# Banded attention in a two-layer decoder kernel: projections in three rounded terms, weights streamed by group, and a new order of the work

## The reference

```python
x = x + _L0_attn_ref(_layernorm(x), wq, wk, wv, wo)

q = einsum('bth,oh->bto', x, wq).reshape(B, T, 16, 128)
k = einsum('bth,oh->bto', x, wk).reshape(B, T, 4, 128)
v = einsum('bth,oh->bto', x, wv).reshape(B, T, 4, 128)
q, k = rope(q), rope(k)
scores = q @ k / sqrt(128)             # keys 128 back at most, none ahead
probs = softmax(scores)
out = (probs @ v).reshape(B, T, 2048) @ wo.T
```

## Time and profile before

| | |
|---|---|
| median of 3 runs | 2411.59 us (2409.08 to 2414.42) |
| the profiled execution | 2406.55 us, span of its trace 2404.8 us |
| attention stage in that trace | 8.6 to 928.6 us |
| busy over the whole span: PE, DVE, ACT, POOL | 89%, 71%, 39%, 44% |
| the same from 0 to 930 us | 92%, 75%, 34%, 38% |

### The profile page before, as it was taken

One profiled execution on the slowest core, in us unless ns is written; L12 is line 12 of the kernel. 1 busy time (PEld: TensorE's weight loads), 2 busy tenths in 40 slices (PEclk: granted clock), 3 DMA queues, 4 the chain that ended last, 5 costly groups with the idle time before them and its releaser, 6 DMA issues. The chain is left out here.

```text
span 2404.8 us, 24923 instructions
## 1 busy us (share of the span) xinstructions
PE 2151.0 (89%) x7344; PEld 1108.7 (46%) x7344; DVE 1712.6 (71%) x2983; ACT 944.7 (39%) x1808; POOL 1048.7 (44%) x798
## 2 busy tenths in 40 slices
PE   6998999899999977997889898999789999999858
PEld 2554445454455543443555555465333433334234
DVE  1787788768876885786889889889546364654554
ACT  1443344333333433764655646465123232332311
POOL 2343354333333440322899998999511011010142
PEclk9999999999999998998999999999889999999979
DMA  7000000000000002455644526353332122221121
GB/s 263 19 19 18 19 20 20 18 18 22 22 18 19 23 23 90 159 186 214 266 162 166 197 105 210 127 203 108 107 80 78 41 77 57 70 70 46 52 109 53
DMA packets 95563, 214.87 MB, mean 89 GB/s; under 512 B 15832, under 2 KB 33112, under 8 KB 93032
## 3 DMA queue, kind: packets, MB, share of 16 engines
q1 hardware_dynamic: 77192, 156.18, 19.8%
q10 hardware_dynamic: 17760, 57.42, 6.7%
q0 software_dynamic: 512, 0.13, 0.0%
HBM read 146.30 MB, written 42.07 MB: 78 GB/s over the span
## 5 line engine op out<-in xcount | busy, mean ns | idle before, releaser
L759 POOL TENSOR_SCALAR a_prob<-a_prob,a_rsum 128x256 f32<-128x256 f32 x256 | 146.6, 590 | 467.3 <-DVE a_rsum L687 467.1
L1455 POOL TENSOR_TENSOR s_state<-s_b_rows,s_delta_u 128x1024 f32<-128x1024 f32 x128 | 303.5, 2384 | 36.9 <-DMA s_b_rows<-scan_bc 34.4
L1499 DVE TENSOR_TENSOR_SCAN s_state<-s_decay,s_state 128x512 f32<-128x512 f32 x256 | 304.9, 1211 | 15.5 <-ACT s_decay L1441 13.2
L1614 PE MATMUL c_bank<-c_xn_parts,c_w_parts 128*128 128x512 f32 (+1 forms) x1056 | 269.5, 405 | 6.2 <-DMA c_w_parts<-ffn_weights_lo 6.2
L1441 ACT ACTIVATE s_decay<-s_delta,s_a 128x512 f32<-128x512 f32 x256 | 173.5, 689 | 226.1 <-DVE s_state L1499 220.6
L491 PE MATMUL a_bank<-a_xn_t,a_wq 128*128 128x512 f32 x512 | 227.3, 592 | 0.0
L602 ACT ACTIVATE a_prob<-a_score,a_neg_m 128x256 f32<-128x256 f32 x256 | 117.6, 475 | 279.0 <-DVE a_neg_m L682 278.8
L1614 PEld LDWEIGHTS c_bank<-c_xn_parts,c_w_parts 128*128 128x128 f32 (+1 forms) x1056 | 196.3, 187 | 65.8 <-issue 20.3
L574 PE MATMUL a_bank<-a_wo,a_out_t 128*128 128x512 f32 x512 | 222.3, 593 | 0.0
L2049 ACT ACTIVATE d_prob_t<-d_score 128x512 f32<-128x512 f32 x256 | 138.9, 595 | 192.2 <-PE d_score L1931 191.1
L373 DVE TENSOR_SCALAR f_picks<-f_mask,f_lut_xor,f_lut 128x260 int32<-128x260 int32 x512 | 202.3, 468 | 9.6 <-DVE f_mask L367 0.5
(11 more groups left out here) (210 smaller groups left out, 3646.2 us busy)
## 6 DMA issues: line engine op xcount, KB each, us to landing
s_b_rows<-scan_bc SPq DMA_DIRECT2D x64, 512.0 KB, 3.7
c_w_parts<-ffn_weights_hi ACTq DMA_DIRECT2D x39, 512.0 KB, 3.6
c_w_parts<-ffn_weights_lo ACTq DMA_DIRECT2D x39, 512.0 KB, 4.5
f_idx<-in_idx SPq DMA_DIRECT2D x64, 130.0 KB, 2.1
ffn_weights<-f_picks SPq DMA_DIRECT2D x64, 130.0 KB, 1.8
d_qs<-d_hi SPq DMA_DIRECT2D x128, 64.0 KB, 2.0
d_ks<-d_hi SPq DMA_DIRECT2D x128, 64.0 KB, 2.0
d_factor<-in_factors SPq DMA_DIRECT2D x16, 512.0 KB, 3.6
```

The lines of the kernel that those rows point to most:

```text
L1455: pool.tensor_tensor(self.state[:, s], row.broadcast_to([P, 2, T]), self.delta_u[:, h % 2], ALU.mult) \
L1499: dve.tensor_tensor_scan(self.state[:, s, e, :], self.decay[u % 2][:], self.state[:, s, e, :], 0.0, ALU.mult, ALU.add).then_inc(self.scann ...
L1614: mm = nc.tensor.matmul(banks[b][0:width[o], :], w_parts[:, n % SLOTS, w, at:at + width[o]], xn_parts[:, x_, k, :], start=((k, w, x_) == t ...
```

## The change

**Split projections.** Wk, Wq and Wv and the transposed x are each held as two float32r parts, the value rounded (`hi`) and what is left (`lo`). A projection into one bank is then 12 float32r matmuls, hi x hi, lo x hi and hi x lo over four row blocks, in place of four float32 ones. Scores, weighting and output product stay float32.

**Streamed weights.** `HeadWeights` holds the parts of one group at a time (five pieces: k and four q; 512 KB with both parts). In the first pass each piece is loaded raw (256 KB, two buffers), rounded by ACT, subtracted by POOL and stored to DRAM by SP; afterwards SP loads the parts of group g + 2 as soon as PE has used those of group g + 1. The values' weights go the same way once. The key's pieces are multiplied by 1/sqrt(128) before rounding, so the exponential loses its scale, and the maximum is taken with its sign turned, so line 682 goes.

**New order.** PE: scores 0 and 1, two projections, scores 2 and 3, three projections, then the output product of the group before (in group 0 the values of this row), then the weighting. In group 3: scores, xn transposes, output of group 2, projections of the next row, weighting, output of group 3. DVE, ACT and POOL follow; the features are now rounded by ACT and subtracted by DVE. The chunks are dealt 4, 4, 3, 5 to the groups. All DMAs of the stage go through SP, in one order with the lookup's. The first pass is unrolled.

```diff
+    GROUPS = (0, 4, 8, 11, PER_PASS)
...
+class HeadWeights:
...
+    def load_piece(self, sp, m, source):
+        if m >= 2:
+            sp.wait_ge(self.split, m - 1)
+        sp.dma_start(self.raw[:, m % 2, :], source).then_inc(self.raw_in[m % 2], 16)
+
+    def load_raw(self, sp, n, p):
+
+        if n:
+            sp.wait_ge(self.stored[p], 16 * n)
+        self.load_piece(sp, self.piece(n, p), self.dram["head_w"][:, n * self.STEPS + p, :])
...
+    def store(self, sp, n):
+        for p in range(self.STEPS):
+            sp.wait_ge(self.ready[p], 16 * (n + 1))
+            sp.dma_start(self.scratch["head_parts"][:, n * self.STEPS + p], self.parts[:, p].bitcast(F32)) \
+                .then_inc(self.stored[p], 16)
...
+    def round(self, act, n, steps):
+        for p in steps:
+            m = self.piece(n, p)
+            if p == 0:
+                raw = self.raw[:, m % 2, :]
+                act.wait_ge(self.raw_in[m % 2], 16 * (m // 2 + 1))
+                self.nc.scalar.activation(raw, raw, ACT.Copy, scale=1.0 / math.sqrt(HD)).then_inc(self.scaled, 1)
+                act.wait_ge(self.scaled, n + 1)
+            self.round_piece(act, m, self.parts[:, p, 0, :])
+
+    def subtract(self, pool, n, steps):
+        for p in steps:
+            m = self.piece(n, p)
+            pool.wait_ge(self.rounded, m + 1)
+            self.nc.gpsimd.tensor_tensor(self.parts[:, p, 1, :], self.raw[:, m % 2, :],
+                                         self.parts[:, p, 0, :].bitcast(F32), ALU.subtract) \
...
-            if g + 1 < KV:
-                order += proj(g + 1)
...
+            if g < LAST:
+                order += proj(g + 1) + (wo_steps(g - 1) if g else v_steps)
             elif more:
-                order += xn_steps + proj(0)
+                order += xn_steps + wo_steps(g - 1) + proj(0)
...
+            def one_pass(i, more):
+                first_pass, last_pass = (isinstance(i, int) and i == at for at in (0, B - 1))
+                for g in range(KV):
+                    chunks = lookup.chunks(g)
+                    ahead = 3 if g == LAST else 1
+                    lookup.sync(sp, i, chunks[:ahead])
+                    if first_pass and g == 0:
+                        for k in range(1, KD):
+                            load_values(k)
+                        load_outputs(0)
+                    if first_pass and g == 1:
+                        for b in range(1, B):
+                            sp.dma_start(x[:, b], dram["x"][b].rearrange("(t p) d -> p t d", p=P)).then_inc(x_in, 16)
+                        load_outputs(2)
+                        load_outputs(3)
+                    if first_pass and g < LAST:
+                        heads.store(sp, g + 1)
+                    if not last_pass or g + 2 < KV:
+                        for p, step in enumerate(proj((g + 1) % KV)):
+                            consumed(ring, i, step)
+                            if first_pass and g < LAST and p == REPS:
+                                lookup.sync(sp, i, chunks[1:2])
+                            if first_pass and g + 2 < KV:
+                                heads.load_raw(sp, g + 2, p)
+                            else:
+                                heads.load_parts(sp, (g + 2) % KV, p,
+                                                 after_stores=KV if first_pass and g + 2 == KV else None)
+                    if first_pass and g == 0:
+                        load_outputs(1)
+                    lookup.sync(sp, i, chunks[2 if first_pass and g < LAST else ahead:])
...
+                for g in range(LAST):
                     scores(i, g, (0, 1))
...
+                    project(ring, i, i, g + 1, proj(g + 1)[0:2])
+                    scores(i, g, (2, 3))
+                    project(ring, i, i, g + 1, proj(g + 1)[2:])
+                    if g:
+                        outputs(i, g - 1)
+                    else:
+                        values(i)
+                    weighted(i, g)
...
-                nc.vector.tensor_reduce(mx[:, h, :], score[h % 2][:], AX_X, ALU.max).then_inc(max_done, 1)
-                dve.wait_ge(max_done, i * HEADS + h + 1)
-                nc.vector.tensor_scalar(neg_m[:, h, :], mx[:, h, :], -scale, None, ALU.mult) \
+                nc.vector.tensor_reduce(neg_m[:, h, :], score[h % 2][:], AX_X, ALU.max, negate=True) \
...
+                for g in range(LAST):
...
                     maxima(i, h)
                     maxima(i, h + 1)
+                    lookup.masks(i, chunks[0])
                     inverse(i, h)
+                    lookup.leaves(i, chunks[0])
+                    rope(*at, proj(g + 1)[0:2])
                     maxima(i, h + 2)
                     inverse(i, h + 1)
                     maxima(i, h + 3)
                     inverse(i, h + 2)
+                    lookup.choose(i, chunks[0])
                     inverse(i, h + 3)
+                    rope(*at, proj(g + 1)[2:4])
...
+                    else:
+                        lookup.pick(i, chunks[1])
+                        rope(*at, proj(g + 1)[4:])
+                    take_output(i, g, 0)
+                    lookup.choose(i, chunks[1])
+                    take_output(i, g, 1)
+                    lookup.pick(i, chunks[2])
+                    take_output(i, g, 2)
+                    take_output(i, g, 3)
...
+                    lookup.choose(i, chunks[2])
+                    for n in chunks[3:]:
+                        lookup.pick(i, n)
+                        lookup.choose(i, n)
```

More of the change, by code:

```diff
@@ L421, in stage_window_attention @@
     v_steps = [("v", tt) for tt in range(TT)]
+    wo_steps = lambda g: [("wo", g, tt) for tt in range(TT)]
+    LAST = KV - 1
     def steps(more):
@@ new lines, in features, with values, weighted @@
+                for k in range(KD):
+                    b, turn = ring.at(("xn", k), i)
+                    act.wait_ge(ring.full[b], turn)
+                    nc.scalar.copy(xn_t[:, 0, k, :], banks[b][:]).then_inc(xn_rounded, 1)
+            def values(i):
+                for tt in (1, 3):
+                    take(("v", tt), i, v[:, tt, :])
+            def weighted(i, g):
+                take(("turn", g, 0, 0), i, prob_t[:, 0, 0, :])
+                take(("turn", g, 1, 0), i, prob_t[:, 1, 0, :])
+                take(("turn", g, 1, 1), i, prob_t[:, 1, 1, :])
+                for tt in range(TT):
+                    take(("pv", g, tt), i, out_t[:, tt, :])
+                    if tt + 2 < TT:
+                        for prev in range(2):
+                            take(("turn", g, tt + 2, prev), i, prob_t[:, tt % 2, prev, :])
@@ L656, in _ @@
[L656 to L659 removed]
+            for p in range(KD - 1):
+                heads.round(act, 1, (p,))
+                swap(first, 0, 0, 0, proj(0)[p + 2:p + 3])
+            heads.round(act, 1, (3,))
             passes(act, one_pass)
@@ new lines, in add, with take_output @@
+            def add(i, g, tt):
+                b, turn = ring.at(("wo", g, tt), i)
+                dve.wait_ge(ring.full[b], turn)
+                nc.vector.tensor_tensor(x[:, i, tt, :], banks[b][:], x[:, i, tt, :], ALU.add) \
+                    .then_inc(ring.free[b], 1)
+            def take_output(i, g, tt):
+                if g:
+                    add(i, g - 1, tt)
+                elif tt % 2 == 0:
+                    take(("v", tt), i, v[:, tt, :])
+            def one_pass(i, more):
+                for g in range(LAST):
+                    at = (ring, i, i, g + 1)
@@ L721, in one_pass @@
-                    lookup.pick(i, g * TT + 1)
-                    lookup.choose(i, g * TT + 1)
-                    for tt in range(TT):
-                        if tt < 2:
-                            lookup.pick(i, g * TT + 2 + tt)
-                            lookup.choose(i, g * TT + 2 + tt)
-                        b, turn = ring.at(("wo", g, tt), i)
-                        dve.wait_ge(ring.full[b], turn)
-                        nc.vector.tensor_tensor(x[:, i, tt, :], banks[b][:], x[:, i, tt, :], ALU.add) \
-                            .then_inc(ring.free[b], 1)
@@ new lines, in one_pass @@
+                maxima(i, h + 1)
+                if more:
+                    features(ring, i, i + 1)
+                inverse(i, h)
+                inverse(i, h + 1)
+                maxima(i, h + 2)
+                maxima(i, h + 3)
+                lookup.masks(i, chunks[0])
+                inverse(i, h + 2)
+                inverse(i, h + 3)
+                lookup.leaves(i, chunks[0])
+                add(i, LAST - 1, 0)
+                lookup.choose(i, chunks[0])
+                add(i, LAST - 1, 1)
@@ new lines, in one_pass @@
+                lookup.pick(i, chunks[1])
+                add(i, LAST - 1, 2)
+                add(i, LAST - 1, 3)
+                lookup.choose(i, chunks[1])
+                if more:
+                    rope(*at, proj(0)[0:2])
+                lookup.pick(i, chunks[2])
+                if more:
```

(14 more changed lines are left out.)

369 lines of the change are left out of this document (227 added, 142 removed).

## The result

The kernel after takes 2436.39 us (median of 4 runs, 2434.19 to 2442.65) against 2411.89 (4 runs) of the kernel before on the same chip: ratio 1.011, 95% interval 1.0088 to 1.0132. It is slower, by 24.5 us or 1.1%; the forecast was 9 us faster, and the measured time lies above the upper end of the range (2430). The profiled execution took 2435.33 us, the span of its trace is 2433.6.

A forecast was written before the change was run, and what follows sets the result against it. PE was taken to bound the pass, DVE next. Start -23.5, first pass +15.9, middle passes -8.1 and last pass +6.6 gave -9.1 us: 2402.5 us from 2411.59, range 2345 to 2430.

The forecast's parts named there:

- rival 1: The forecast itself: waits for sums and ropes eat PE's saving; 2382 to 2416 us, chance 0.50.
- The first pass loses: Pass 0: weight splitting and SP's single order delay groups 0 and 1; 239.5 us, 15.9 more than before.
- The bound: Limits of the first-pass term: nothing lost (219), or 30 us if large issues hold SP as they held ACT.
- The start: Row 0's part, before pass 0: pass 0 begins at 37.4 instead of 60.95, 23.5 us off.
- The steady passes: The two middle passes: 219.3 us each, PE's saving returning as waits; together they win 8.1 us.
- the last pass: The final pass, now including its row's values: 204.0 against 197.4 us, 6.6 more.
- the choose keeps its 3.0: DVE's choose step in the lookup: stays at 3.0 us beside POOL's operations.
- rival 4: POOL also stops DVE's choose: 1.2 us more in 13 groups, 16 us, 2418; chance 0.08.
- Rival 3: SP's order becomes the bound if indices land after T + 27.7: 22 us over 15 groups, 2425; chance 0.15.
- Rival 2: DVE meets less of POOL and indices are in time: groups 47.8 us, group 3 65; 2357, chance 0.27.
- The turn of the sign: DVE's removed negation of the maximum: 64 x 373 ns busy, only some 0.2 us of each on the path.

The follow-up runs named there:

- e3: Kernel after with the second chunk's indices loaded early in passes 1 to 3 and the third and fourth sums ahead of the third chunk's pick: 2389.06 us.
- e4: Kernel after with four float32 matmuls on the rounded parts instead of twelve float32r ones, leaving out the lower-part products: 2441.39 us.
- e13: e10 with the values' weights rounded and subtracted ahead of the work they stood behind, in group 0 of pass 0: 2362.85 us.
- e10: Kernel after with only issue orders changed: sums ahead of the third pick, indices earlier in every pass, last-group ropes of q1 to q3 together: 2358.11 us.
- e6: Kernel after with pass 0's second-chunk indices behind the second raw piece and third-chunk indices ahead of the fifth: 2428.11 us.
- e1: Kernel after with the second chunk's indices loaded ahead of the last three weight loads in passes 1 to 3: 2425.24 us.
- e5: Kernel after with the maximum and its negation as two DVE instructions again: 2445.57 us.
- e12: e3 with the maximum and its negation as two DVE instructions again: 2394.78 us.
- e9: Kernel before with the new order alone, plus third and fourth sums ahead of the third pick and last-group ropes of q1 to q3 together: 2355.81 us.

## Why the prediction was wrong, by its own steps

**What held.** Its rival 1 mechanism is the right one: PE's saving comes back as waits for sums and ropes. A float32r pair takes 5.95 us (forecast 2.80 + 2.96 = 5.76), indices land at T + 26.6 (T + 26), the fourth sum ends at T + 42.3 (41.3), the group ends at 51.3 (50.8). Moving the sums and the indices frees it (e3), and more PE time leaves it as it was (e4).

**What failed: "The first pass loses", a term of +15.9 us that measured +36.4** (260.0 against 223.6). It holds 20.5 of the 38.9 us between the forecast of the stage (-9.1) and the trace (958.41 - 928.59 = +29.8). Group 0 was to take 65 us and took 78.7, group 1 56 and took 60.5. The chain of group 0 was in the prediction, but the prediction names no stores there, and the head of the chain is sized as if the five ahead of the raw pieces cost nothing. Stores of that size, here and in row 0's part, land 4.6 to 10.0 us after issue. SP stands 4.5 us for the first of them, and the first raw piece reaches ACT 5.6 us after issue, where I had reckoned 2.6. So POOL's second subtraction, forecast for T + 35, ends at T + 41.7, and the indices behind it are there at T + 45.0.

From there the delay goes once around the engines. DVE's rope of q3 stands behind the pick that needs the indices; PE's last value bank waits for that rope; ACT's rounding stands behind its copy of that bank; POOL's subtraction waits for ACT, SP's fifth piece for POOL, and the third chunk's indices stand behind the piece: asked for at T + 58.5 instead of T + 49 and, behind 1 MB of wo, there only at T + 64.2. DVE's copy of a value bank waits for them, and PE for the copy. Beside this chain the values' weights came at T + 33.4 instead of T + 28, by the order of ACT and POOL (e13 changes it, and that wait goes).

No run removes the stores alone; that they are the head of the chain is read from these waits and from e10's indices. e6 takes the indices out of their place behind the raw pieces, and its groups 0 and 1 take 66.5 and 56.9 us. That these are near the forecast's 65 and 56 is chance: they are of another kernel.

The bound was wrong too. I had given 30 us as the most that this term could lose, from ACT's 1 MB issues alone, not from a chain that is late at its head; 36.4 is beyond it.

**The start**: 42.9 instead of 37.4, 5.5 us, with the same missing term. The first group's parts are stored ahead of the second group's raw pieces, and a store of 512 KB lands 7.3 us after issue (median of 20). The first raw piece behind them, issued at 29.22, reaches ACT at 34.88. DVE's timeline shows the hole: 7.8 us for a swap that waits for a rounding that waits for the load.

```profile
37.39 0.69 DVE L854 TENSOR_TENSOR a_q_t<-a_bank,a_cos 128x512 f32<-128x512 f32 x1 [7.80 <-ACT a_rope_b L769]
```

**The steady passes**: 224.0 and 225.2 instead of 219.3, together 10.6 us, and the last pass 2.2. That is 0.5 to 1.9 us a group. The five float32r banks took 0.4 us more (5.95 + 8.74 where I had 5.76 + 8.56), but e4 shows that PE's time there is not on the path; what is, is DVE, slowed by POOL more than I allowed: in group 1 its fourth sum ends 1.0 us late. The group of the predicated copies answers to "the choose keeps its 3.0":

```profile
L394 DVE COPY_PREDICATED f_picks<-f_mask,f_picks 128x260 int32<-128x260 int32 x448 | 196.3, 498 | 20.7
```

498 ns each against 456 before, 18.6 us of DVE in the stage, or 0.3 us for a choose of seven; in the steady group 3.69 us for seven instead of 3.01. The row that I went by had POOL's last operation just over. So rival 4 is a real effect, at up to somewhat over half its price there (0.7 us where I gave 1.2). The Trainium skill (SBUF — State Buffer, Who interferes with whom) has the rule: a VectorE instruction with two SBUF inputs contends with a GpSimd instruction that reads SBUF. The trace agrees for the copies (3.69 us beside POOL, 3.01 with it idle). It also shows the leaves, each reading one mask, going from 2.69 to 6.02 and 6.87 us for eight; the page has that for the modes with two ports, which no view here names.

**Rival 3** (SP's order becomes the bound, decided once indices land later than T + 27.7) did not come true in the steady passes, where the indices are there by T + 26.8 and e1 takes 0.2 to 3.8 us off a group. In the first pass it did: in group 0 the indices landed at T + 45. The forecast had them there only as a part of its +15.9. I gave it 0.15 with a price per steady group, and its place was wrong.

**Rival 2** needed that DVE meets less of POOL; its predicated copies got slower instead. The turn of the sign, put at 0.2 us of each head on the path, measured about 0.13 (e5, e12).

## What to carry to other kernels

When a change both reorders a pipeline and makes one engine's work cheaper, measure the order alone: here it gives 25 us (53 with two more moves in DVE's order), while the cheaper matmuls, with the weights streamed for them, are worth 4 us a pass with the orders put right and cost over 50 in all as delivered. In an engine's stream, put what another engine needs next (a sum that frees a bank, a rope) ahead of work that nobody waits for; one moved line was worth 36 us. And in a queue that everything shares, count the stores ahead of a load too, and follow a late transfer around the loop of engines until it comes back: here 7 us at the head of the chain were 14 at the end of the group.

## What was not expected

- Eight leaves of 128x260 take 2.69 us with POOL idle and up to 6.87 beside its operations, so that a wait for data and a wait for POOL can stand in for each other (e1).
- The stages after the attention run unchanged code and took 1469.0 to 1485.6 us from the next stage's first matmul to the end, in 14 profiled executions. The cause is open; it limits what whole times say of edits of a few us.
- PE's granted clock follows its waits: 0.89 in the long first pass, 0.95 in the steady passes of the kernel after, 1.00 in e9, where PE is busy 208.1 of 210.1 us. The twelve-matmul bank is priced at full clock; part of what a wait costs comes behind it, as in the 10.76 us that 36 matmuls took after the 9.4 us wait in group 0 (granted clock 0.77), where e13 has 8.63 for the same 36 after a wait of 0.56 (clock 1.00).
